# Adaptive-layernorm transformer, second attention layer: score product ahead of the product of the maxima in TensorE's order

## What is computed

```python
def _L1_attn_ref(x, W_qkv, b_qkv, W_proj, b_proj):
    ...
    qkv = x @ W_qkv + b_qkv
    ...
    alibi = jnp.minimum(idx[None, :] - idx[:, None], 0).astype(jnp.float32)
    bias = slopes[:, None, None] * alibi
    scale = 1.0 / math.sqrt(D)
    scores = jnp.einsum('bhtd,bhsd->bhts', q, k) * scale + bias[None]
    w = jax.nn.softmax(scores, axis=-1)
    y = jnp.einsum('bhts,bhsd->bhtd', w, v)
    y = y.transpose(0, 2, 1, 3).reshape(B, T, C)
    return y @ W_proj + b_proj
...
h = _layernorm(x, axis=-1) * (1 + ca) + sa
x = x + ga * _L1_attn_ref(h, L1_attn_W_qkv, L1_attn_b_qkv, L1_attn_W_proj, L1_attn_b_proj)
```

## Time and profile before

| | us |
|---|---|
| median of 3 runs | 1060.96 |
| lowest and highest | 1057.96, 1062.22 |
| profiled execution | 1063.57 |
| its span | 1061.8 |
| PE busy in the span | 947.9 |
| DVE busy | 783.9 |
| ACT busy | 753.1 |
| POOL busy | 536.7 |

### The profile page before, as it was taken

How to read it: one execution, slowest core, us unless ns; L and a number is a source line. 1 busy time by engine, 2 the same in 40 slices (tenths; PEclk the granted TensorE clock), 3 DMA queues, 4 the chain that set the end, 5 groups by cost and what they waited for, 6 DMA issues and landing times. The chain is left out here.

```text
span 1061.8 us, 23047 instructions
## 1 busy us (share of the span) xinstructions
PE 947.9 (89%) x8688; PEld 519.1 (49%) x8688; DVE 783.9 (74%) x1324; ACT 753.1 (71%) x1380; POOL 536.7 (51%) x748
## 2 busy tenths in 40 slices
PE   5788789889898999999999989999999999899896
PEld 3333334333344888888877733333333333333564
DVE  4777767778792676766677768888898888895465
ACT  2477677778776666566555469888888888888663
POOL 3465655675553022213210148785867778666344
PEclk8699999999999999999999989999999999999999
DMA  6323412211202733333322110212112020200011
GB/s 177 110 82 87 136 51 86 79 50 41 84 15 55 186 93 101 90 91 109 111 83 87 52 52 30 75 32 64 31 54 73 14 74 26 70 11 16 23 31 50
DMA packets 63582, 73.91 MB, mean 70 GB/s; under 512 B 14120, under 2 KB 45992, under 8 KB 63088
## 3 DMA queue, kind: packets, MB, share of 16 engines
q1 hardware_dynamic: 62608, 71.66, 23.4%
q10 hardware_dynamic: 864, 0.79, 0.4%
HBM read 39.24 MB, written 2.77 MB: 40 GB/s over the span
## 5 line engine op out<-in xcount | busy, mean ns | idle before, releaser
L862 ACT ACTIVATE at_E<-at_Sb 128x512 f32<-128x512 f32 x832 | 445.6, 599 | 81.2 <-PE at_Sb L715 75.7
L926 DVE TENSOR_REDUCE mx<-at_Mb 128x2 f32<-128x1024 f32 x242 | 281.9, 1217 | 43.0 <-PE at_Mb L678 41.8
L763 PE MATMUL at_Ob<-at_E,VP 128*32 128x256 f32 (+2 forms) x2816 | 213.9, 377 | 16.6 <-ACT Oev L890 10.4
L715 PE MATMUL at_Sb<-QP,KP 64*128 64x512 bf16 (+3 forms) x1024 | 204.5, 347 | 10.4 <-ACT full_k L417 3.6
L1028 POOL TENSOR_TENSOR at_E<-at_E,factor 128x512 f32<-128x512 f32 x128 | 162.4, 1273 | 76.8 <-ACT at_E L862 66.8
L678 PE MATMUL at_Mb<-KP,QP 62*128 62x512 bf16 x996 | 174.5, 356 | 18.0 <-DVE mx L926 15.4
L929 DVE TENSOR_REDUCE mx<-at_Mb 128x2 f32<-128x768 f32 (+1 forms) x128 | 138.4, 1087 | 57.0 <-PE at_Mb L678 55.7
L1039 POOL TENSOR_SCALAR_AFFINE_SELECT at_E<-at_E 128x512 f32<-128x512 f32 x128 | 82.7, 659 | 76.4 <-ACT at_E L862 76.4
L763 PEld LDWEIGHTS at_Ob<-at_E,VP 128*32 128x32 f32 x2816 | 57.1, 108 | 119.7 <-issue 88.1
L715 PEld LDWEIGHTS at_Sb<-QP,KP 64*128 64x128 bf16 x1024 | 74.9, 96 | 72.3 <-ACT at_E L862 36.1
L1468 DVE TENSOR_TENSOR ex_hh<-ex_R,ex_th 128x512 f32<-128x512 f32 x88 | 64.5, 733 | 60.1 <-ACT ex_th L1406 59.4
(11 more groups left out here) (207 smaller groups left out, 1446.2 us busy)
## 6 DMA issues: line engine op xcount, KB each, us to landing
QP<-q SPq DMA_DIRECT2D x96, 128.0 KB, 2.4
KP<-k SPq DMA_DIRECT2D x90, 128.0 KB, 2.4
ex_R<-rw_dram SPq DMA_DIRECT2D x32, 256.0 KB, 3.9
ctxN<-Oev SPq DMA_DIRECT2D x16, 256.0 KB, 3.0
denB<-rdram SPq DMA_DIRECT2D x64, 64.0 KB
ex_R<-rw_dram SPq DMA_DIRECT2D x16, 224.0 KB, 4.1
ex_R<-rw_dram SPq DMA_DIRECT2D x16, 192.0 KB, 3.6
ex_R<-rw_dram SPq DMA_DIRECT2D x16, 160.0 KB, 3.5
```

The source lines that it names most:

```text
L715: return pe.matmul(out[:, at:at + SEQ - q0], KP[p0:p0 + ROWS_H, b % 2, 2 * g + a, kt * P:(kt + 1) * P], QP[p0:p0 + ROWS_H, b % 2, 2 * g + ...
L763: last = pe.matmul(Ob[VW * i:VW * (i + 1), 0, q0:q1], weights_of(b, G, kt, i, q0), moving, start=(kt == 0 and q0 == 0), stop=False, skip_g ...
L862: nc.scalar.activation(dst, src, ACT.Exp).then_inc(s["s_read"], 1)
L926: v.tensor_reduce(mx[:, G % 2, :, t % 2, t // 2], src, AX.X, ALU.max).then_inc(s["m_read"], 1)
```

## The change

In the second attention every beat of TensorE's loop has the two score products first, the product of the maxima second and the values third. In the first attention the order stays.

```diff
@@ -795,10 +795,14 @@
             for beat in range(START, END):
+                if not causal:
+                    for _, G, t, c in slots_S(beat):
+                        key_score(G, t, c)
                 if m_of(beat) is not None:
                     max_score(*m_of(beat))
-                for _, G, t, c in slots_S(beat):
-                    key_score(G, t, c)
+                if causal:
+                    for _, G, t, c in slots_S(beat):
+                        key_score(G, t, c)
                 for G, off in zip(*chunks(beat)):
                     values(G, off)
                 for name in fills(beat):
```

## The result

| | before | after |
|---|---|---|
| median us (4 runs each, same chip) | 1061.59 | 1073.42 |
| lowest and highest | 1057.96, 1069.25 | 1071.66, 1075.06 |
| ratio, 95% interval | | 1.0093, 1.0066 to 1.0121 |
| profiled span | 1061.8 | 1069.9 |
| second attention layer, from ScalarE's table load to the last context read | 369.28 | 380.49 |

The change makes the kernel slower by 9.9 us (1.0093 x 1061.59; the interval is 7.0 to 12.8). The forecast was +5.9 on a median of 1060.96, range 1057 to 1072. By the ratio the changed kernel stands at 1060.96 x 1.0093 = 1070.8, inside the range; the plain median, 1073.42, belongs to four runs whose own before is 1061.59, and lies 1.4 us above the range's upper end. Slower was the likeliest of the three outcomes, at 0.45. The sign holds and so does most of the working; one cost was missed altogether, and it is nearly as large as the whole forecast.

A forecast was written before the change was run, and what follows sets the result against it. No engine was full; TensorE, ScalarE and VectorE were close to it and held each other up. Fills +5.9, VectorE's stretch +1.1 and GpSimd's cover -1.1 made +5.9 us: 1060.96 to 1066.9, range 1057 to 1072.

The forecast's parts named there:

- The step from M to V: TensorE's beat: from maxima product (M, L678) to values product (V, L763), taken as 0.31 us, ends 0.22 and 0.40.
- Stretches over a plain V: From ScalarE's release of a score product (S) over a values product (V) to the next S: 1.55 before, 1.54 after.
- The waits before the reads: ScalarE's waits before reading q, k and values: near 0.86 for 0.64, 0.37 for 0.15, 0.79 for 0.57.
- its stretch: Once a batch VectorE is the path, from a maxima product to the output projection; it was to enter 0.44 later.
- The cover by GpSimd: After the q and k splits GpSimd's factor product comes late, hiding 0.19 in six batches: -1.1 us.
- The wrong step: VectorE's run from 828.25 to 838.25, layer statistics included, was taken as gapless; entering 0.44 later, net +0.22, five batches, +1.1.
- The exit's -0.22: At the output projection, end of VectorE's run, the score product comes at once, 0.22 sooner, in five batches.
- the transpose's +0.22: The fill that transposes the normalised rows starts 0.22 later; counted in 6 of its 7 places.
- The clock: Near 734 TensorE's granted clock falls; with scores ahead it may not stand idle, giving back 2.3 us: 1064.6.
- The moved window: Rival: the fills' 0.22 vanish in hidden slack, 0 to 2 us more, 1059 to 1063; chance 0.22.
- The faster case: Rival: score products stop waiting for VectorE, 50 x 0.22 = 11.0 us less, 1050, limit 1027; chance 0.13.
- The larger loss: Rival: maxima products wait behind waiting scores, VectorE becomes the path in the fill region, 8.4 on top, 1075; chance 0.10.

The follow-up runs named there:

- j: Changed kernel with VectorE's aggregation, negated means and variance plus epsilon (L364 to L368) one beat later, 19 for 18: 1067.83 us for 1063.03, ratio 1.0039.
- c: Kernel before, with the new order only in beats that end in a fill (values, transpose, q, k): 1066.49 us, ratio 1.0036.
- g: Kernel before, with the new order only in beat 23, the one behind the output projection: 1061.59 us for 1063.03, ratio 0.9978.
- d: Changed kernel with the two small operations L367 and L368 of the second layer issued by GpSimd, not VectorE: 1064.99 us, ratio 1.0024.

## Why the prediction was right in direction and short by four microseconds

**Right.** The step from M to V, of which no row was to be had, is 0.31, and the beat is unchanged at 1.10. Stretches over a plain V come out even: ScalarE's work is the same and no gain shows anywhere. The waits before the reads were forecast 0.86, 0.37 and 0.79 and are 0.87, 0.32 and 0.79. One reason given for the 0.31 does not hold, though: if sharing rows of the array kept a load from overlapping, S to M could not take 0.22 either. In the trace of after M's loads, on the rows of the S ahead of them, start at 834.36 while that S runs (834.35 to 834.73), and M starts 0.22 behind it. What makes the step to V longer, 0.31, no run shows. VectorE enters its stretch 0.44 later, to the hundredth. The cover by GpSimd is real: ScalarE starved 0.21 for the S at 856.89, behind the values of the earlier trace rows, and no longer does, so that 0.22 more at the values are only 0.03 in the period.

**The wrong step** is the sentence that VectorE "works on without a gap (layer statistics lie in it)". I took its instructions as fixed and moved them as a block by 0.44. But the block moved against GpSimd's, which hangs on ScalarE and stayed, and the statistics slid from just ahead of a factor product into it. That is 0.79 in each of six batches, 4.7 us, and perhaps 1.0 at the end of the layer. 5.9 + 4.7 + 1.0 would have been 11.6 on the layer, which grew by 11.2. Both instructions stood in the trace of before, 0.10 us apart, and I had quoted neither.

**Two terms that cancel.** The exit's -0.22 and the transpose's +0.22 are both in the sum, 5 and 6 times. They are one M: overtaken at the exit, and owed when the chain from the output projection comes to the transpose. With the hold gone hT stands at +0.40 (j), the entry alone; with the fill's order alone it is +0.19 (c), and with the exit's alone -0.04 (g), since the next beat collects it. The sum was right here.

**By its size** the order's own cost was forecast as 46.07 to 47.0 and is 46.88. Without the hold in the batches the answer would have been some 1066 (j is 4.1 us above before by its ratio, 1061.59 + 4.1), beside a forecast of 1066.9.

**The clock** was to give back 2.3 us perhaps. It gave nothing. The batch at 734 keeps its clock: VectorE is later now and no longer waits for the reciprocal's DMA. But behind the hold TensorE stands idle instead. In the first batches of the changed kernel (windows, then two of TensorE's waits just ahead of them):

```profile
650.00:652.00 2.00, 2.00 (x28) 1.05 (x28) 2.00 (x2) 0.42 (x1) 1.76 (x3) 0.57 0.03 8
652.00:654.00 2.00, 2.00 (x15) 0.39 (x16) 1.01 (x2) 1.09 (x2) 0.25 (x1) 0.58 0.00 0
699.00:702.00 3.00, 3.00 (x20) 1.90 (x12) 1.71 (x3) 0.00 (x0) 1.03 (x1) 0.59 0.02 5
```

```profile
648.69 0.39 PE L678 MATMUL at_Mb<-KP,QP 62*128 62x512 bf16 x2 [1.08 <-DVE mx L930]
649.82 0.39 PE L678 MATMUL at_Mb<-KP,QP 62*128 62x512 bf16 x2 [0.52 <-DVE mx L930]
```

A mean of 0.57 to 0.59 is the lower level (1.2 GHz) for most of the window. The waits ahead, 1.08 and 0.52, stand behind the hold of VectorE, in every batch, and the clock falls in two of them. In j and d, without the hold, no fall comes after the stage's first microseconds, and in c the one fall comes behind the one hold. So the hold brings falls with it; what decides in which batch wasn't found.

**The rivals.** The moved window is out: the waits grew and the period with them. The faster case is out: ScalarE's 50 waits became 41 of a larger sum, 40.6 us for 34.1. The larger loss had nearly the right time, 1075, and the wrong reason: it had M behind a waiting S make VectorE the path in the fill region. Were that so, the fill region, from hT to the next values, would have grown by a reduction, and it grew by 0.41; and j and d, which leave TensorE's order alone, could not have taken back 0.82 and 1.11 per batch.

## What to carry to other kernels

When a change delays one engine's queue against another's, don't move the block as if its durations were its own. Look in the trace at what the other engine does in the moved place, and above all at VectorE's tensor_scalars and two-input instructions on SBUF, however small, beside long GpSimd ones. A lengthened instruction is no wait, and lists of waits don't have it; compare the mean durations and the busy time of an engine whose work has not changed. A wait that an order removes is only a gain if the instruction which was overtaken isn't owed again before the next starved engine; follow it until it is paid. A step put ahead of a fill costs its own length at each fill where somebody starves, and less where another wait lies behind.

## What the runs showed of the hardware

A tensor_scalar of VectorE on 128x4 numbers takes 0.17 us alone and 0.96 or 1.26 when it starts 0.34 or 0.04 us behind a GpSimd product of 128x512 in SBUF that takes 1.27: it ends with the product. Started 0.10 ahead, it costs neither of them anything; started 0.02 ahead, as the last of the four at 962.68 in the changed kernel is, it is held as well (1.38 for 0.34). The hold goes both ways, and it also strikes instructions with two SBUF inputs. In the kernel before the product behind the normalisation takes 1.41, and the context's scaling takes 1.06 for the usual 0.68 beside another product:

```profile
925.37 1.41 POOL L1028 TENSOR_TENSOR at_E<-at_E,factor 128x512 f32<-128x512 f32 x1 [0.99 <-PE at_Sb L715]
```

```profile
971.08 1.27 POOL L1028 TENSOR_TENSOR at_E<-at_E,factor 128x512 f32<-128x512 f32 x1
971.84 1.06 DVE L321 TENSOR_TENSOR ctxT<-ctxN,denB 128x512 f32<-128x512 f32 x1 [2.82 <-DMA denB<-rdram]
```

A product of the changed kernel that starts 0.06 behind the context's scaling takes 1.75 (at 979.29). Reductions from PSUM beside the same products stay at 1.2. The Trainium skill ("SBUF — State Buffer", Who interferes with whom) has these cases, the tensor_scalar, the instruction with two SBUF inputs and the reduction; the runs agree with it on each.

Not held beside such products are VectorE's aggregation (L364, 0.15 to 0.17), its statistics (L356, 0.28) and its reciprocal (L302, 0.54), which have one SBUF input each.
